# A Mamba layer between two expert layers on one core: the slot plan laid out anew, long steps in parts, tokens on partitions, decays by pairs

## The reference, cut to what matters

```python
x = x + 0.5 * ffn(layernorm(x))      # 8 experts, top 2, and a shared expert
x = x + mamba(layernorm(x))          # in-projection, causal conv of 4 taps, scan over 16 states
x = x + 0.5 * ffn(layernorm(x))      # the same FFN weights again

# ffn, xf of shape (8192, 128), E = 8 experts of H = 176, shared width 352
top_logits, idx = top_k(xf @ Wg, 2);  probs = softmax(top_logits)
w = zeros(n, E).at[arange(n)[:, None], idx].add(probs)
h = silu(einsum('tc,ech->eth', xf, W1)) * einsum('tc,ech->eth', xf, W2)
y = einsum('eth,ehc,te->tc', h, W3, w) + (silu(xf @ Ws1) * (xf @ Ws2)) @ Ws3

# mamba, d_inner = 256, d_state = 16, r the layer's input
x_in, z = split(r @ W_in + b_in);  xc = silu(conv(x_in))
Bm, Cm = split(xc @ W_xp + b_xp);  delta = softplus(xc @ W_dt + b_dt)
h = exp(delta * A) * h + delta * xc * Bm        # for each token in turn
y = einsum('bds,bs->bd', h, Cm) + D_skip * xc
r2 = r + (y * silu(z)) @ W_out + b_out;  out = alpha * (r2 - mean) / (std + 1e-6) + beta
```

## Time and profile before

| | |
|---|---|
| runs (3) | median 2236.86 us, 2232.0 to 2238.75 |
| profiled execution | 2241.29 us, its span 2239.5 us |
| busy, share of the span | PE 80%, DVE 73%, ACT 69%, POOL 64% |
| mean granted TensorE clock | 0.887 of full speed |
| ACT_TABLE_LOAD | 227 at line 680 and 217 at line 657, 1283 ns each |
| chain that ended last, by engine | PE 43%, ACT 21%, DVE 17%, issue 12%, POOL 3% |

### The profile page before, as it was taken

How to read it: one execution, slowest core, us unless ns; L and a number is a source line. 1 busy time by engine, 2 the same in 40 slices (tenths; PEclk the granted TensorE clock), 3 DMA queues, 4 the chain that set the end, 5 groups by cost and what they waited for, 6 DMA issues and landing times.

```text
span 2239.5 us, 22836 instructions
## 1 busy us (share of the span) xinstructions
PE 1794.9 (80%) x4674; PEld 804.4 (36%) x4674; DVE 1639.6 (73%) x2505; ACT 1535.3 (69%) x2083; POOL 1441.3 (64%) x1286
## 2 busy tenths in 40 slices
PE   3878587979888888887888798788888878885577
PEld 1433233434334333333433343333333433332233
DVE  2257878687786878878687877878778786879742
ACT  1257587777778767786876778687677867776522
POOL 3346676666667675776767666676766676676753
PEclk9989788989898898998989898898989889897698
DMA  4117565555556555555555654655556555557642
GB/s 130 45 55 178 119 164 130 144 133 143 127 142 153 130 135 134 152 132 151 152 137 129 152 143 127 151 147 140 130 131 159 131 145 138 133 122 173 150 111 61
DMA packets 119129, 300.05 MB, mean 134 GB/s; under 512 B 19184, under 2 KB 40400, under 8 KB 104656
## 3 DMA queue, kind: packets, MB, share of 16 engines
q0 software_dynamic: 18432, 125.84, 28.1%
q1 hardware_dynamic: 92672, 168.88, 24.2%
q10 hardware_dynamic: 7888, 4.09, 0.7%
HBM read 167.67 MB, written 5.24 MB: 77 GB/s over the span
## 4 chain that ended last, share of the span: by engine, by line
PE 43%; ACT 21%; DVE 17%; issue 12%; POOL 3%; ACTq 1%; DMA 1%; DVEq 0%; POOLq 0%
PE ps_y L1043 9%; PE ps_h2a L1048 6%; DVE hist L868 5%; PE ps_m L1003 5%; ACT L680 5%; PE ps_h1a L1030 4%; PE ps_h1b L1030 4%; ACT L657 4%; PE ps_h2b L1048 4%; DVE den L912 3%; ACT decay L657 3%; ACT silu L680 2%; DVE yacc L950 2%; PE ps_m L1110 2%; DVE ps_db L834 2%
## 5 line engine op out<-in xcount | busy, mean ns | idle before, releaser
L569 POOL TENSOR_TENSOR prod<-hist,crow 128x1024 f32<-128x1024 f32 x224 | 556.0, 2482 | 371.8 <-DVE hist L868 368.0
L1043 PE MATMUL ps_y<-gated,down_w 128*128 128x512 f32 (+1 forms) x896 | 517.6, 664 | 101.3 <-POOL gated L521 63.2
L868 DVE TENSOR_TENSOR_SCAN hist<-decay,ps_db 128x1024 f32<-128x1024 f32 x256 | 583.2, 2278 | 13.8 <-issue 11.3
L521 POOL TENSOR_TENSOR gated<-gated,silu 128x512 f32<-128x512 f32 x352 | 476.3, 1416 | 138.1 <-DVE gated L860 108.4
L834 DVE TENSOR_TENSOR ps_db<-du,ps_db 128x1024 f32<-128x1024 f32 x256 | 313.7, 1225 | 319.1 <-PE ps_db L1012 318.8
L657 ACT ACTIVATE decay<-delta,a_neg 128x510 f32<-128x510 f32 x512 | 338.1, 711 | 2.6
L1048 PE MATMUL ps_h2a<-xnT,up_w 128*128 128x512 f32 (+1 forms) x448 | 253.2, 649 | 53.3 <-DVE gated L860 53.3
L680 ACT ACT_TABLE_LOAD x227 | 291.2, 1283 | 5.5 <-issue 0.7
L1043 PEld LDWEIGHTS ps_y<-gated,down_w 128*128 128x128 f32 (+1 forms) x896 | 180.3, 209 | 319.3 <-issue 218.0
L1030 PE MATMUL ps_h1a<-xnT,up_w 128*128 128x512 f32 (+1 forms) x448 | 248.0, 636 | 49.7 <-ACT silu L680 48.8
L657 ACT ACT_TABLE_LOAD x217 | 278.4, 1283 | 3.8
(11 more groups left out here) (137 smaller groups left out, 2242.5 us busy)
## 6 DMA issues: line engine op xcount, KB each, us to landing
...
crow<-c_rows SPq DMA_DIRECT2D x128, 512.0 KB, 4.2
...
```

The lines of the kernel that those rows point to most:

```text
L521: nc.gpsimd.tensor_tensor(gated[:, pos % NGATE, :], gated[:, pos % NGATE, :], silu[:, (pos + NCHUNK * f_parity(k, f)) % NSILU, :], ALU.mul ...
L569: nc.gpsimd.tensor_tensor(prod[:, (pair - 1 + odd) % 2, s % 2, :, :], hist[:, s % 2, :, :], c_all, ALU.mult).then_inc(prod_done, 1)
L868: nc.vector.tensor_tensor_scan(hist[:, s % 2, :, :].rearrange("p h t -> p (h t)"), decay[:, s % NA, :, :, :].rearrange("p h b t -> p (h b ...
L1043: nc.tensor.matmul(ps_y[:], down_w[0:rd, jd, :], gated[0:rd, posd % NGATE, :], start=(posd == 0), stop=(posd == NCHUNK - 1)).then_inc(down ...
```

## The change

It does these things together:

1. **New slots.** `UNIT` gives each chunk its slot: the second FFN in slots 1 to 9, 11, 12, 14, 15 and 16, the first in slots 18 to 31. `unit` looks over the end of an iteration, so the first FFN's last chunks are gated, joined and multiplied by `down_w` in slots 0 to 3 of the next iteration. `PLAN` and `SP_PLAN` are laid out anew. The steps in `EARLY` (`addy0`, `addy1`, `resid`) stand ahead of the scan in their slot on DVE.
2. **Long steps in parts.** The convolutions are cut in two (`in0a`, `in1a`), as is `gate_y`; `du` is taken from `delta`, the copy of the logits from `route`, POOL's part of each statistics step (`scale`) from DVE's, `ln_norm` in four steps, the softplus in `sp_exp` and `sp_ln`.
3. **The router's weights on POOL.** DVE ends with `hot`; the softmax of two and `wtok` are seven POOL instructions.
4. **Tokens on partitions.** The down projection and the out-projection take `gated` and `yacc` as stationary, in four tiles of 128 tokens, and move 128 columns of weights. `ps_y` then has tokens on partitions, and DVE adds it to x directly: `y`, `yT`, `outT` and their tiles go. The bias of the out-projection is added by one bf16 matmul of three parts, made once at the start by eight small DVE instructions.
5. **Decays by pairs.** ACT makes the decays of two states in slots 0, 4, ..., 24, and those of the next group's first two in slot 28.
6. **`x1n` by a DMA.** The normalised x of the Mamba layer's input stays in one of two tiles, and SP copies it to `rtok` (`keep_x1n`) in place of ACT's second normalisation.

```diff
     PLAN = {
-        0: ["stats0", "y0"], 1: ["yT0", "x1n"], 2: ["addy0", "norm0"], 3: ["stats2", "fold"], 4: ["xT0"],
-        5: ["logits0", "norm2"], 6: ["route0", "gate_y"], 7: ["xT2"], 8: ["weights0", "outproj"], 9: ["in0"],
-        10: ["wT0"], 11: ["outT"], 12: ["resid"], 13: ["in1", "stats3"], 14: ["in2"],
-        15: ["in3", "ln_norm"], 17: ["y1"], 18: ["dt0", "stats1"], 19: ["dt1"], 20: ["yT1", "norm1"],
-        21: ["addy1"], 22: ["xproj", "delta"], 23: ["bparts"], 24: ["xT1"], 25: ["logits1"], 26: ["route1"],
-        27: ["cT"], 28: ["bT", "weights1"], 30: ["wT1"],
+        0: ["stats0"], 1: ["scale0"], 2: ["norm0"], 3: ["fold"], 4: ["addy0", "xT0"], 5: ["stats2", "scale2", "logits0"],
+        6: ["norm2", "rcopy0"], 7: ["gate_y0", "xT2"], 8: ["gate_y1"], 9: ["outproj"], 10: ["resid", "in0a"],
+        11: ["in0", "route0"], 12: ["stats3", "in1a"], 13: ["in1", "scale3"], 14: ["in2", "ln_norm"],
+        15: ["in3", "ln_scale"], 16: ["weights0"], 17: ["dt0"], 18: ["wT0", "ln_shift"], 19: ["dt1", "ln_add"],
+        20: ["sp_exp"], 21: ["addy1", "xproj", "stats1"], 22: ["scale1", "sp_ln", "bparts"], 23: ["norm1", "cT"],
+        24: ["bT", "delta"], 25: ["xT1"], 26: ["logits1"], 27: ["rcopy1", "route1"], 28: ["du"], 29: ["weights1"],
+        31: ["wT1"],
     }
-    UP1, UP0, BACK = 0, 14, 4
+    EARLY = ("addy0", "addy1", "resid")
+    UNIT = {s: (1, pos) for pos, s in enumerate((1, 2, 3, 4, 5, 6, 7, 8, 9, 11, 12, 14, 15, 16))}
+    UNIT.update({18 + pos: (0, pos) for pos in range(NCHUNK)})
+    GATE, JOIN, BACK = 1, 2, 4
-    DECAYS = {2 * s - 4: s for s in range(2, NS)}
+    DECAYS = {4 * i: (2 * i + 2, 2 * i + 3) for i in range(NS // 2 - 1)}
+    def unit(k, odd, slot, lag):
+        back = slot < lag
+        if slot - lag + back * SLOTS not in UNIT:
+            return None
+        f, pos = UNIT[slot - lag + back * SLOTS]
+        of, parity = (k - 1, 1 - odd) if back else (k, odd)
+        return (of, parity, f, pos) if (last(of) if f else enters(of)) else None
...
# POOL
+                        elif step == "weights0" and enters(k) or step == "weights1" and tail(k):
+                            chain.link(nc.gpsimd.tensor_tensor(drop[:], top[:, :, 1], top[:, :, 0], ALU.subtract))
+                            chain.link(nc.gpsimd.tensor_tensor(edrop[:], euler[:], drop[:], ALU.pow))
+                            chain.link(nc.gpsimd.tensor_tensor(den[:], edrop[:], pow_mone[:], ALU.subtract))
+                            chain.link(nc.gpsimd.tensor_tensor(prob[:, :, 0], den[:], pow_mone[:], ALU.pow))
+                            chain.link(nc.gpsimd.tensor_tensor(prob[:, :, 1], edrop[:], prob[:, :, 0], ALU.mult))
...
# ACT
-                    if slot == SLOTS - 1 and lead(k):
+                    if slot == SLOTS - 4 and lead(k):
                         decays(k + 1, nxt, range(NA // 2))
                     elif slot in DECAYS and scans(k):
-                        decays(k, odd, [DECAYS[slot]])
+                        decays(k, odd, DECAYS[slot])
...
# DVE
-                            dve.wait_ge(edrop_ready, route_no(k, step) + 1)
-                            chain.link(nc.vector.tensor_scalar(den[:], edrop[:], 1.0, None, ALU.add))
-                            chain.link(nc.vector.reciprocal(prob[:, :, 0], den[:]))
-                            chain.link(nc.vector.tensor_tensor(prob[:, :, 1], edrop[:], prob[:, :, 0], ALU.mult))
+                            dve.wait_ge(down_done, fcount(k if f else k - 1, f, NCHUNK, NCHUNK))
+                            xr = xres[:, oldest if f else ahead, :, :].rearrange("p t c -> p (t c)")
+                            nc.vector.scalar_tensor_tensor(xr, ps_y[:], 0.5, xr, ALU.mult, ALU.add
+                                                           ).then_inc(y_taken, 1)
...
# PE
-                        nc.tensor.matmul(ps_y[:], down_w[0:rd, jd, :], gated[0:rd, posd % NGATE, :], start=(posd == 0),
-                                         stop=(posd == NCHUNK - 1)).then_inc(down_done, 1)
+                        for t in range(TILES):
+                            ins = nc.tensor.matmul(ps_y[:, t * C:(t + 1) * C],
+                                                   gated[0:rd, posd % NGATE, t * P:(t + 1) * P], down_w[0:rd, jd, :],
+                                                   start=(posd == 0 and t == 0),
+                                                   stop=(posd == NCHUNK - 1 and t == TILES - 1))
+                        ins.then_inc(down_done, 1)
...
# SP
+                        elif step == "keep_x1n" and scans(k):
+                            sp.wait_ge(norm_ready[2], k + 1)
+                            if tail(k):
+                                sp.wait_ge(mamba_added, k)
+                            sp.dma_start(rtok[:], x1n[odd][:]).then_inc(x1n_ready, 16)
```

288 lines of the change are left out of this document (143 added, 145 removed), and 8 rows, old and new, of the table SP_PLAN.

## The result

The changed kernel takes **2150.8 us** (median of 4 runs, 2146.4 to 2161.9) against 2234.4 for the one before on the same chip (2231.7 to 2238.8): a ratio of 0.963, interval 0.960 to 0.966. It is faster by 3.7%, where 11.5% had been forecast; the time lies above the range. The profiled execution has a span of 2146.8 us.

A forecast was written before the change was run, and what follows sets the result against it. Bound: each state's busiest engine, summed. Full iterations from 132 to 114 us, twelve times, -216; lighter iterations -36; filling and draining -4: 2241.3 becomes 1985 profiled, 1981 as median. Predicted 1980, range 1890 to 2120 us.

The forecast's parts named there:

- The bound is the sum of the maxima: Full iteration: the busiest engine of each of sixteen states, added, gives its length; 128.9 of 133.0 us before.
- The factor 0.95: Full iteration: scales the table of maxima, 139.6 against 133.0 measured before, so 117.0 becomes 111.5 us after.
- outproj behind gate_y1, +1.5: One slot apart: PE waits, then DVE waits for 2.2 us of out-projection and B; +1.5 us a full iteration.
- wT0 and wT1 behind POOL, +1: PE's wT0 and wT1 wait for a POOL chain of 4 us two slots behind; +1 us a full iteration.
- Port contention: gate_y in slots 7 and 8: cut pieces may each be caught anew, some 2 us; 3.50 was simply halved.
- Decays by pairs: ACT, full iteration: 15 of 33 table loads go, 19.2 us; block of 5.4 us costed at nothing, at most 11.
- The down projection: PE, per chunk: eight passes of 128 columns take 0.90 us against 0.86, +1.1 us an iteration.
- Rival A: PE's down projection: weight loads do not hide, some 142 us an iteration, 2360 us; chance 7%.
- Rival B: Full iterations: new waits take half the gain as all engines are nearly full, 124 us, 2111 us; chance 18%.
- The lighter iterations: Four lighter iterations with scans: table 392 against 436, a tenth less of 404.4 us, taken as 36 us.
- keep_x1n and the SP queue: SP: keep_x1n holds store_x and later rows, costed at nothing; without cover, gates of slot 25 on would wait.
- The signs: Right: iterations 110 to 118 us, no state over 10, clock 0.93, ps_db wait halved; wrong: iteration over 124.

The follow-up runs named there:

- a11: Changed kernel with delta and du both back in slot 23, next to bparts, instead of slots 24 and 28: 2134.4 us, ratio 0.957.
- a12: a8 with delta and du both in slot 23, as in a11: 2066.9 us, ratio 0.925.
- a10: Changed kernel with the second half of gate_y back in slot 7 behind the first, outproj staying in slot 9: 2132.4 us, ratio 0.954.
- a5: Changed kernel with five of the seven router weight operations, den to wtok, back on DVE in slots 16 and 29: 2138.3 us, ratio 0.955.
- a7: a6 with the next iteration's first row of B sent ahead of wT1 on PE: 2082.3 us, ratio 0.931.
- a13: Changed kernel with three of four down-projection column blocks left out in every second chunk, output incomplete: 2149.4 us, ratio 0.961.
- a1: Changed kernel with outproj in slot 10 instead of 9, resid, the convolutions, in2 and in3 one slot later: 2085.1 us, ratio 0.931.
- a2: Changed kernel with weights0 on POOL in slot 12 instead of 16: 2107.9 us, ratio 0.944.
- a6: Changed kernel with both moves, outproj in slot 10 and weights0 in slot 12: 2078.5 us, ratio 0.928.
- b1: The kernel before with decays by pairs alone, in slots 0, 4, ..., 24: 2225.7 us, ratio 0.996.
- a4: Changed kernel with the decays of states 2 to 15 one by one again, in every even slot: 2184.6 us, ratio 0.975.
- a3: Changed kernel with the down projection in its old form, two passes of 512 columns a chunk: 2139.7 us, ratio 0.957.
- a8: a6 with SP's store of x behind the FFN weight rows, in slot 29, and each row one slot earlier: 2066.9 us, ratio 0.925.
- a9: Changed kernel with only SP's store of x moved to slot 29 and each FFN weight row one slot earlier: 2153.4 us, ratio 0.963.

## Why the prediction was right or wrong

**Direction: right. Size: wrong, by 171 us.** Of the profiled difference of 163 between forecast (-256) and measurement (-93), 130 are the full iterations (124.8 for 114, twelve times), 35 the lighter ones, and filling and end were 1 better than the 4 forecast; the rest of the 171 is how the medians lie to the profiled executions.

**"The bound is the sum of the maxima": the step that failed.** The prediction priced a full iteration as the plan's sum of maxima times 0.95 plus two waits, and so made levelling the states worth its full difference in maxima. It read the bound from before, where in nearly each state one engine was as long as the interval. a11 and a12 show that a state 4 us longer is given back by the next three; in a10, a5 and a7 what one state lost its neighbour for the most part took. a13 shows the reverse: 4.8 us less of busy time on PE, which is the busiest engine in most states, changed nothing. The observation was right, and the reading was not: that an engine is full in a state says that it used the time, since PE runs ahead on the FFN when it can. What costs is a loop in which nobody can run ahead, as in state 4, and a stretch in which POOL falls behind, as in state 9.

**The factor 0.95, and what levelling was worth.** Taken for all twelve full iterations, the busiest engine of each state adds up to 127.9 us of 132.0 before and to 117.0 of 124.8 after; the prediction's table had 139.6 and 117.0. For the uneven kernel the table put 11.7 us too much, and 0.95 corrected that. The level kernel needed no such correction, and the factor took 5.5 us off a sum that was right: in part by luck, since state 8 has 4.1 for the table's 8.4 and state 9 has 12.0 for 7.6. Over the maxima stand 7.8 us of waits, 4.1 of them in state 4, where the prediction allowed 2.5: 5.3 more. These two, 5.5 and 5.3, are the 10.8 us by which an iteration missed 114. Said the other way, levelling lowered the maxima by 10.9 us and not by 22.6, and waits grown from 4.1 to 7.8 took back 3.7, which leaves the 7.2 measured. The likely reason for the first, not shown by an edit of the kernel before, is that its engines already ran ahead of their slots.

**The new waits: right place, wrong size.** "outproj behind gate_y1, +1.5" measured 5 (a1); the term left out that gate_y1's second half runs at 2.71 us beside POOL's prod, and that PE, after 3.99 us of idle time, ran the out-projection at a granted clock of 0.62 and then 0.50, 3.7 us before it came to the row of B, not 2.2 with B included. "wT0 and wT1 behind POOL, +1" measured 3.6 by the medians and 4.7 by the profile for weights0 (a2): not the wait of `wT0` alone (1.23 in the rows above) but what stands behind the chain on POOL, a prod and two multiplications, which PE and through it DVE wait for. The two overlap, 5.5 together by the profile and 6.0 by the medians (a6).

**Port contention.** The two products of gate_y took 3.19 us a half (L964's mean 1.455 and L967's 1.732), against the forecast's 2.36. From the exclusive port pair of the Trainium skill ("SBUF — State Buffer", SBUF: two separate sides) the prediction had worked out that each cut piece could be caught anew, for some 2 us in all. The rows agree: the two halves came out 1.7 us longer together, and L967 took 0.69 us at its shortest and 2.72 at its longest. The prediction noted this and took the lower value.

**Decays by pairs: costed at nothing for the block, rightly, but the ACT time was credited wherever ACT had been the longest.** In the changed kernel PE waits 4 us in all for silus. ACT's 14 table loads, 18 us an iteration, gave 8 us of the whole in the old layout (b1; 0.7 an iteration by the medians, 2.3 by the profiles, of which the one before, 2241.3 us, was slower than any run timed with it), and cost 34 when taken back from the new (a4; 2.5 by the profiles, 2.8 by the medians).

**The down projection: right.** 0.89 us for eight passes against 0.90. Rival A is refuted by the row and by a3; its 142 us were also some 3 too high by its own figures (121 at a clock of 0.87 is 139). The rule of the Trainium skill ("TensorE: Matmul & The Clock Gate", Part 3) that a weight load overlaps only matmuls of another row group would, by the prediction's estimate, have given 1.73; the measurement decides, and in this kernel loads of full height hide behind the pass before.

**Rival B** forecast 124 us an iteration and 2111. The iteration is the one that came, by another mechanism: not "full everywhere" (POOL has 91.5 of 120.4, 76%), but two places. The rest of the distance from 2111 to 2151 is 25 us that B still took off the lighter iterations, 10 in the full ones, and some 5 in filling, end and the distance of the median from the profiled execution.

**The lighter iterations: wrong by 35, mostly open.** Their table was scaled from the full ones. Even in a8 they take 399.0. State 4 is 12.2 to 12.3 us in three of the four, the same loop; with it gone (a1) the sum is 399.2, so the loop is 4 of the 35. Why the rest did not come was not separated.

**keep_x1n and the SP queue: right in the changed kernel** (a9: nothing), and the sentence on what is late next was right as well: the gates of the last slots waited for their rows, and cost 12 us once the cover went (a6 against a8). The part of SP's list that did it was the store of x, together with the one slot by which the rows behind it came earlier.

**The signs.** State over 10: yes, two. An iteration over 124 us: yes. 18 table loads: yes, in iteration 8. Clock 0.93 or more: 0.94 in the full iterations, 0.91 over the whole. 0.11 apart: yes. DVE's wait for ps_db halved: it rose to 400, the clearest sign against.

What part of the change brought its 7 us an iteration is settled for the pairs alone: 0.7 to 2.8, by the layout they stand in. The form of the down projection (a3), the place of the weights (a5), the split of gate_y (a10) and the spread of delta and du (a11) each seem to cost something, 11 to 18 us of the whole by the medians, taken alone; that is about the spread of the changed kernel's own runs (15 us), though none of the runs overlap. The new places of the chunks, and x1n, y and the transposes no longer there, were not undone separately; the other 4 us and more lie among them.
